# Weight preparation of a transformer block on eight cores: modulation weights in 1 MB slabs spread over the layer norm, the down-weight fold between attention heads, transposes behind them

## The chip, the cores and the metric

The program runs on all eight cores of one Trainium2 chip. Each core computes one of eight batch entries and holds its own copy of the weights; the cores don't exchange data. The metric is the device time of the slowest core in microseconds. A profile shows one execution, on the slowest core.

## The reference

One block: attention and a gated feed-forward part, each behind a layer norm that is modulated by a vector computed from `c`.

```python
mod = (_silu(L0_c) @ L0_wmod).reshape(8, 6, 1, -1)
sa, ca, ga, sb, cb, gb = (mod[:, k] for k in range(6))
ga = (2 * (ga >= 0) - 1) * jnp.maximum(jnp.abs(ga), 0.25)
gb = (2 * (gb >= 0) - 1) * jnp.maximum(jnp.abs(gb), 0.25)
h = _layernorm(x) * (1 + ca) + sa
x = x + ga * attention(h, w_qkv, w_out)      # 16 heads of 128, S = D = 2048
h = _layernorm(x) * (1 + cb) + sb
x = x + gb * ffn(h, gate_w, up_w, down_w, router_w1, router_w2)
# ffn: (silu(h @ gate.T) * (h @ up.T) * top-16-of-64 block mask) @ down.T, I = 8192
```

All inputs are float32; `wmod` is 2048 x 12288 (96 MB), `gate_w`, `up_w` and `down_w` are 64 MB each, `w_qkv` 48 MB, `w_out` 16 MB.

## The kernel before

The program is one long function, `build_nc`, that appends instructions to five lists, one per engine (TensorE "pe", ScalarE "act", VectorE "dve", SyncE "sp", GpSimd "gp"). Each engine works its list strictly in order; what stands later waits for what stands earlier. `b.wait` puts a semaphore wait into an engine's list. `b.dma(queue, ...)` issues a transfer from SP ("sp"), GpSimd ("gp") or ScalarE ("sc"); it first waits for the transfer that used the same of its queue's channels (7, 5 and 4, in turn), so at most that many are in flight per queue. Casts from float32 to bfloat16 in a DMA are issued by GpSimd. Eight PSUM banks are handed over by `bank_acquire`, `bank_written`, `bank_read` and `bank_read_done`.

The stages, in program order:

1. *Modulation* (L311 to L348). 24 column blocks of 512, each in 8 tiles of 256 rows: GpSimd loads a tile of `wmod` (512 KB of float32) into a ring of six, TensorE multiplies it with `silu(c)` (L338), VectorE copies the row into `mod_raw` (L343). After block 7, `replicate` (L290) spreads `ca` and `sa` over 128 partitions by a matmul with ones (L298). Behind it come the casts of `w_qkv` and `w_out` (L353, L355), the signs and magnitudes of `ga` and `gb` (L362 to L373), their way through `vec_scr` in HBM into `ga_cols` and `gb_cols`, and `cb1_rep` and `sb_rep`.
2. *First layer norm* (L437 to L461). 16 tiles of `x`, in groups of four: load, sum and squares, small statistics, then scale, shift and a transpose by TensorE (L426, copied out at L432).
3. *Casts* of `gate_w` and `up_w` to bfloat16 in HBM (L465 to L469), 32 of 4 MB, issued by GpSimd.
4. *The fold* (L474 to L489): `down_w` times `gb`, in 256 steps of 128 x 512. SP loads `wdf_in` (two buffers), VectorE multiplies (L486), GpSimd stores to `wd_bf`. In VectorE's list all 256 stand ahead of the first head.
5. *Preps* (L499 to L526), on SP alone: 192 pairs of a DMA transpose into `prep_buf` (from `wg_bf`, `wu_bf`, `wd_bf`) and a scatter to `wgT`, `wuT` or `wdT`. Each waits for the one ahead.
6. *Attention* (`emit_head`, L528), 16 heads. Every second head loads V weights and computes V (L546) for two heads; each head loads and computes Q and K (L569), then runs four quarters: scores (L594), exponentials on ScalarE (L603), the product with V (L617), and on VectorE the reciprocal and the scaling (L624, L627). The next quarter's scores can start only when VectorE has freed the four banks of the last one. The weight loads are issued by ScalarE.
7. *Output projection* (L660), the second sum and statistics (L684 to L707).
8. *Feed-forward part* (from L709). SP loads `router_w1` (L713); at L747 VectorE and ScalarE wait for all preps; then four strips of 512 tokens (L897, L904, L950).

Of the kernel before, what the change touches and what calls it, by code (L numbers as in the profile page):

```python
# [128 lines left out]
def build_nc(phases=4, taps=(), debug_sync=False):  # L129
# [95 lines left out]
    mod_raw = fv(A, 0, 12288, parts=1)  # L225
# [62 lines left out]


    def replicate(row_ap, dst_ap, dep_val, banks=(2, 3), plus1=False):  # L290
        last = None
        for j in range(4):
            bk = banks[j % 2]
# [15 lines left out]
        return last

    mm_t = {}  # L311
    mod_evac = []
    tile_idx = 0
    for nb_ in range(24):
        bk = nb_ % 2
        b.bank_acquire(bk)
        for kcp in range(8):
            slot = tile_idx % 6
            if tile_idx >= 6:
                b.wait("gp", "pe", mm_t[tile_idx - 6])  # L320
            src_ap = wmod_h[2 * kcp * 128:(2 * kcp + 2) * 128,
                            nb_ * 512:(nb_ + 1) * 512]
            src_ap = src_ap.rearrange("(two p) j -> p two j", p=128)
            dst_ap = wmod_ring[:, slot * 1024:(slot + 1) * 1024]
            dst_ap = dst_ap.rearrange("p (two j) -> p two j", two=2)
            t_d = b.dma("gp", dst_ap, src_ap)
            b.wait_tok("pe", t_d)
            if nb_ == 0 and kcp == 0:
                b.wait("pe", "act", t_siluc)
            for sub in range(2):  # L330
                kc = 2 * kcp + sub
                mm_t[tile_idx] = b.op(
                    "pe", lambda e, o=bank(bk)[0:1, :],
                    l=silu_cb[:, kc:kc + 1],
                    r=wmod_ring[:, slot * 1024 + sub * 512:
                                slot * 1024 + sub * 512 + 512],
                    s=(kc == 0), p=(kc == 15):
                    e.matmul(o, l, r, start=s, stop=p), "pe")  # L338
            tile_idx += 1
        b.bank_written(bk)  # L340
        b.bank_read("dve", bk)
        t = b.op("dve", lambda e, d=mod_raw[0:1, nb_ * 512:(nb_ + 1) * 512],
                 s=bank(bk)[0:1, :]: e.tensor_copy(d, s), "dve")  # L343
        b.bank_read_done("dve", bk)
        mod_evac.append(t)
        if nb_ == 7:
            t_ca1 = replicate(mod_ca, ca1_repA, mod_evac[7], plus1=True)
            t_sa = replicate(mod_sa, sa_repA, mod_evac[7])  # L348

    cast_order = [0, 2, 4, 1, 3, 5]  # L350
    cast_qkv_t = [None] * 6
    for ch in cast_order:
        cast_qkv_t[ch] = b.dma("gp", wqkv_bf[:, ch * 1024:(ch + 1) * 1024],  # L353
                               wqkv_h[:, ch * 1024:(ch + 1) * 1024])
    cast_wout_t = [b.dma("gp", wout_bf[:, ch * 1024:(ch + 1) * 1024],  # L355
                         wout_h[:, ch * 1024:(ch + 1) * 1024]) for ch in range(2)]

    sgn_scr = fv(R2, 0, 1024)[0:1, :]
    sgn2 = fv(R2, 2048, 1024)[0:1, :]
    abs_scr = fv(R2, 4096, 1024)[0:1, :]  # L360
    abs2 = fv(R2, 6144, 1024)[0:1, :]
    for row_base in (4096, 10240):  # L362
        for hf in range(2):
            seg = mod_raw[0:1, row_base + hf * 1024:row_base + (hf + 1) * 1024]
            b.op("dve", lambda e, r=seg: e.tensor_scalar(
                sgn_scr, r, 0.0, 2.0, OP.is_ge, OP.mult), "dve")
# [5 lines left out]
            b.op("dve", lambda e: e.tensor_scalar(abs2, abs_scr, 0.25, None, OP.max), "dve")
            b.op("dve", lambda e, r=seg: e.tensor_mul(r, sgn2, abs2), "dve")  # L373
    cb1_row = fv(R2, 0, 2048)[0:1, :]
    t_modpost = b.op("dve", lambda e: e.tensor_scalar(cb1_row, mod_cb, 1.0, None, OP.add), "dve")

    b.wait("act", "dve", t_modpost)
    t1 = b.dma("sc", vec_scr[0:1, :], mod_ga)
    t2 = b.dma("sc", vec_scr[1:2, :], mod_gb)
    b.wait_tok("sp", t1)  # L380
    b.wait_tok("sp", t2)
    b.dma("sp", ga_cols, vec_scr[0:1, :].rearrange("a (k p) -> (a p) k", p=128),
          slow_ok=True)
    t_gbcols = b.dma("sp", gb_cols,
                     vec_scr[1:2, :].rearrange("a (k p) -> (a p) k", p=128),
                     slow_ok=True)


    t_cb1 = replicate(cb1_row, cb1_rep, t_modpost)
    t_sbr = replicate(mod_sbv, sb_rep, t_modpost)  # L390

# [98 lines left out]
    t_wdfold = wdf_out_t[255]  # L490

    wgT_v = wgT_h.rearrange("(ic p dc) j -> ic p dc j", ic=NB, p=128)
    wuT_v = wuT_h.rearrange("(ic p dc) j -> ic p dc j", ic=NB, p=128)
    wdT_v = wdT_h.rearrange("(g c p s) j -> g c p s j", g=4, c=NB, p=128)
# [3 lines left out]
    last_scat = 0  # L498
    b.wait("sp", "dve", wdf_ts_t[255])  # L499
    for name, src_bf, dstv in (("wg", wg_bf, wgT_v), ("wu", wu_bf, wuT_v)):  # L500
        for dcq in range(NDC):
            for qu in range(4):
                need_ch = ((qu + 1) * 2048 - 1) // 512
                b.wait_toks("sp", [cast_t[(name, ch)] for ch in range(need_ch + 1)])
                b.wait_tok("sp", last_scat)
                t_tp = b.dma("sp", prep_buf,
                             src_bf[qu * 2048:(qu + 1) * 2048,
                                    dcq * 128:(dcq + 1) * 128],
                             transpose=True)
                b.wait_tok("sp", t_tp)  # L510
                dst = dstv[qu * 16:(qu + 1) * 16, :, dcq, :].transpose([1, 0, 2])
                src_ap = prep_buf.rearrange("p (ic j) -> p ic j", ic=16)
                last_scat = b.dma("sp", dst, src_ap)
                prep_gu_toks.append(last_scat)
        prep_t[name] = last_scat
    b.wait_toks("sp", wdf_out_t)
    for cq in range(NB):
        b.wait_tok("sp", last_scat)
        t_tp = b.dma("sp", prep_buf, wd_bf[:, cq * 128:(cq + 1) * 128],
                     transpose=True)  # L520
        b.wait_tok("sp", t_tp)
        dst = wdT_v[:, cq, :, :, :].transpose([1, 0, 2, 3])
        src_ap = prep_buf.rearrange("p (g s j) -> p g s j", g=4, s=4)
        last_scat = b.dma("sp", dst, src_ap)
        prep_wd_toks.append(last_scat)
    prep_t["wd"] = last_scat  # L526
# [537 lines left out]
```

How the kernel before makes its waits and increments, by code:

```python
        def f(e, sem=sem, val=val):  # L51
            e.wait_ge(sems[sem], val)
# [4 lines left out]
    def op(self, eng, fn, sem=None, n=1):  # L57
        if (self.debug_sync and eng in OWN_ALL) or eng in self.AUTO_SELF:
            own = OWN_ALL[eng]
            val = self.cnt[own]
            if val > 0:
                sems = self.sems
                self.emit(eng, lambda e, own=own, val=val:
                          e.wait_ge(sems[own], val))
        if sem is None:
            self.emit(eng, lambda e, fn=fn: fn(e))
            return None
        self.cnt[sem] += n
        tgt = self.cnt[sem]
        sems = self.sems
        def f(e, fn=fn, sem=sem, n=n):
            fn(e).then_inc(sems[sem], n)
        self.emit(eng, f)
        return tgt
```

## Time and profile before

| | us |
|---|---|
| median of the runs shown | 8954.16 (8994.57 and 8913.74) |
| the profiled execution, its own time | 8727.57 |
| span of its slowest core (core 4) | 8726.0 |
| spans of the eight cores | 8653.6 to 8726.0 |
| TensorE busy | 5271.0 (60%) |
| VectorE, ScalarE busy | 1438.4, 1057.0 |
| mean granted TensorE clock | 0.789 of full speed |

A span runs from the first to the last instruction of a core. The busy share is an average over stages that differ much, so the stages are read one by one. DMA share is the mean busy share of the core's 16 DMA engines. The two runs without a profile took some 2 to 3% longer than the profiled one.

### The profile page before, as it was taken

How to read it: one execution, taken by the hardware profiler on the slowest of the kernel's cores; microseconds unless marked ns; L12 is line 12 of the kernel's file. 1: busy time of each engine (PE TensorE's matmuls, PEld its weight loads, DVE VectorE, ACT ScalarE, POOL GpSimd, SP SyncE). 2: the span in 40 equal slices, each digit the busy share in tenths (PEclk: the TensorE clock that was granted, in tenths of full speed). 3: DMA queues.
4: the chain of work that ended last, by engine and by line, in shares of the span. 5: the costliest groups of instructions: out<-in, count | busy, mean ns of one | idle time of the engine just before them, and what ended most of it. 6: DMA issues, size and time to landing. Idle time of an engine off the chain costs nothing.

```text
span 8726.0 us, 77823 instructions; the slowest of 8 cores (8653.6 to 8726.0 us)
## 1 busy us (share of the span) xinstructions
PE 5271.0 (60%) x25265; PEld 2409.3 (28%) x25265; DVE 1438.4 (16%) x2507; ACT 1057.0 (12%) x1239; POOL 301.3 (3%) x499
## 2 busy tenths in 40 slices
PE   5410011006666676666615888768886888858888
PEld 0000010003433444433202333323333333323333
DVE  0152001220000000001044211131102212031110
ACT  0010000003433333431110000000000000000000
POOL 3200001220000000000000000000000000000000
PEclk8555556558888888887856999879997899979999
DMA  9999996566666655300021223322232222422234
GB/s 130 141 148 118 109 110 146 175 182 128 128 127 130 130 129 143 94 10 15 22 80 49 106 102 115 117 77 102 102 127 76 106 102 102 140 68 102 102 111 135
DMA packets 1158830, 945.75 MB, mean 108 GB/s; under 512 B 791666, under 2 KB 1021106, under 8 KB 1152178
## 3 DMA queue, kind: packets, MB, share of 16 engines
q1 hardware_dynamic: 945408, 672.28, 27.1%
q0 software_dynamic: 83632, 184.59, 15.8%
q10 hardware_dynamic: 129412, 83.91, 3.5%
q8 instruction: 228, 3.74, 0.2%
q14 instruction: 150, 1.23, 0.1%
HBM read 839.97 MB, written 251.67 MB: 125 GB/s over the span
## 4 chain that ended last, share of the span: by engine, by line
PE 53%; DMA 15%; DVE 11%; another core or an unknown queue 7%; issue 7%; ACT 5%; DVEq 1%; ACTq 0%; POOLq 0%; POOL 0%; SPq 0%
PE PS L897 13%; PE PS L950 10%; PE PS L904 10%; PE PS L569 6%; DMA wd_bf<-A 4%; ACT A L603 4%; DMA R<-wmod 4%; PE PS L660 3%; PE PS L617 3%; DMA A<-wqkv_bf 2%; PE PS L546 2%; DMA R<-x 2%; PE PS L594 2%; DVE dout_tile L916 2%
## 5 line engine op out<-in xcount | busy, mean ns | idle before, releaser
L897 PE MATMUL PS<-A 128*128 128x512 bf16 x4096 | 1119.1, 435 | 5.9 <-DMA A<-wgT 5.8
L950 PE MATMUL PS<-R,A 128*128 128x512 bf16 x4096 | 916.2, 387 | 51.1 <-DMA A<-wdT 31.9
L904 PE MATMUL PS<-A 128*128 128x512 bf16 x4096 | 925.8, 379 | 0.0
L594 PE MATMUL PS<-A 128*128 128x512 bf16 x1024 | 376.0, 475 | 879.9 <-DVE R L627 661.1
L603 ACT ACTIVATE A<-PS,cexp 128x1024 bf16<-128x1024 f32 x512 | 616.7, 1204 | 944.2 <-PE PS L594 904.9
L569 PE MATMUL PS<-R,A 128*128 128x512 bf16 x2048 | 514.7, 418 | 283.6 <-DMA A<-wqkv_bf 283.6
L897 PEld LDWEIGHTS PS<-A 128*128 128x128 bf16 x4096 | 426.2, 109 | 648.4 <-issue 336.0
L546 PE MATMUL PS<-A,R 128*128 128x256 bf16 x2048 | 241.0, 283 | 577.6 <-DMA A<-wqkv_bf 576.4
L950 PEld LDWEIGHTS PS<-R,A 128*128 128x128 bf16 x4096 | 406.2, 100 | 558.4 <-issue 96.9
L904 PEld LDWEIGHTS PS<-A 128*128 128x128 bf16 x4096 | 400.7, 98 | 483.4
L916 DVE TENSOR_TENSOR dout_tile<-silu_sb,PS 128x512 bf16<-128x512 bf16 x256 | 176.1, 688 | 1835.7 <-PE PS L904 1777.1
L911 ACT ACTIVATE silu_sb<-PS 128x512 bf16<-128x512 f32 x256 | 152.9, 597 | 2517.0 <-PE PS L897 2444.0
L594 PEld LDWEIGHTS PS<-A 128*128 128x128 bf16 x1024 | 103.5, 103 | 1109.8 <-issue 1047.7
L546 PEld LDWEIGHTS PS<-A,R 128*128 128x128 bf16 x2048 | 207.3, 102 | 610.5 <-issue 579.1
L569 PEld LDWEIGHTS PS<-R,A 128*128 128x128 bf16 x2048 | 214.0, 106 | 580.1 <-issue 385.0
L860 PE MATMUL PS<-mask_fm,id64b 64*1 64x512 bf16 x256 | 105.7, 413 | 444.0 <-DVE R L921 441.5
L617 PE MATMUL PS<-A 128*128 128x129 bf16 x4096 | 334.4, 251 | 31.5 <-ACT A L603 31.5
L624 DVE RECIPROCAL inv<-PS 128x1 f32<-128x1 f32 x256 | 43.1, 168 | 1845.0 <-PE PS L617 1824.8
L617 PEld LDWEIGHTS PS<-A 128*128 128x128 bf16 x4096 | 316.5, 115 | 65.2 <-issue 57.5
L660 PE MATMUL PS<-R,A 128*128 128x512 bf16 x1024 | 267.5, 421 | 67.6 <-DMA A<-wout_bf 66.9
L486 DVE TENSOR_SCALAR A<-A,gb_cols 128x512 bf16<-128x512 f32 x256 | 124.7, 487 | 1075.3 <-DMA wd_bf<-A 1071.2
L338 PE MATMUL PS<-R,silu_cb 128*1 128x512 bf16 x384 | 192.9, 608 | 168.1 <-DMA R<-wmod 156.3
(125 smaller groups left out, 2416.6 us busy)
## 6 DMA issues: line engine op xcount, KB each, us to landing
A<-wgT SPq DMA_DIRECT2D x256, 512.0 KB, 3.6
A<-wuT SPq DMA_DIRECT2D x256, 512.0 KB, 4.5
A<-wdT SPq DMA_DIRECT2D x128, 1024.0 KB, 5.4
A<-down_w SPq DMA_DIRECT2D x256, 256.0 KB, 3.0
R<-wmod POOLq DMA_DIRECT2D x192, 256.0 KB, 8.6
wg_bf<-gate_w POOLq DMA_DIRECT2D x16, 2048.0 KB, 97.4
wu_bf<-up_w POOLq DMA_DIRECT2D x16, 2048.0 KB, 96.9
wd_bf<-A POOLq DMA_DIRECT2D x256, 128.0 KB, 3.0
```

Of the source, the lines that this page charges most:

```text
L338: e.matmul(o, l, r, start=s, stop=p), "pe")
L546: e.matmul(o, l, r, start=s, stop=p), "pe")
L569: e.matmul(o, l, r, start=s, stop=p), "pe")
L594: e.matmul(o, l, r, start=True, stop=True), "pe")
L603: e.activation(d, s, AF.Exp, bias=cexp[:, 0:1], scale=cexp[:, 1:2]), "act")
L617: e.matmul(o, l, r, start=s, stop=p), "pe")
L660: e.matmul(o, l, r, start=s, stop=p), "pe")
L897: e.matmul(o, l, r, start=s, stop=p), "pe")
L904: e.matmul(o, l, r, start=s, stop=p), "pe")
L911: e.activation(silu_sb, s, AF.Silu), "act")
L916: e.tensor_mul(dout_tile, silu_sb, s), "dve")
L950: e.matmul(o, l, r, start=s, stop=p), "pe")
```

## The change

The change reorders the preparation of weights and vectors.

- The modulation is computed in six groups of 2048 columns, each in 16 slabs of 128 rows x 2048 columns (1 MB of float32). The ring has two slots. A slab feeds four matmuls into four banks (L304). `repl_from_banks` copies each bank's row to a bounce buffer and replicates it; `gagb_post` does signs and magnitudes straight from the banks, in four pieces, each stored through `vec_scr` from ScalarE's queue.
- `sa` and `ca` (32 slabs) come first. The 32 slabs of `ga` and `sb` stand in the layer norm, two behind each tile of `x`. The 32 of `cb` and `gb` follow, with three casts of `w_qkv` between them. The other casts come behind slab 95.
- The fold becomes `wdf_step`, 20 steps behind each head from head 2 on. Its store is issued by SP, no longer by GpSimd.
- The preps become `emit_preps`, called behind the last head and the last fold step.

```diff
-    for nb_ in range(24):
-        bk = nb_ % 2
-        b.bank_acquire(bk)
-        for kcp in range(8):
-            slot = tile_idx % 6
...
+    def mod_slab_dma(idx):
+        if idx >= 2:
+            b.wait("gp", "pe", slab_mm[idx - 2])
+        g, kc = divmod(idx, 16)
+        slab_tok[idx] = b.dma("gp", ring_slot(idx),
+                              wmod_h[kc * 128:(kc + 1) * 128,
+                                     g * 2048:(g + 1) * 2048])
...
+            b.wait("act", "dve", b.cnt["dve"])
+            if q > 0:
+                b.wait_tok("act", toks[q - 1])
+            b.op("act", lambda e, s=src: e.activation(abs_scr, s, AF.Abs), "act")
...
+    for idx in range(16):
+        mod_slab_dma(idx)
+        mod_slab_mms(idx)
+    t_bounce_pe = repl_from_banks(sa_repA, False, 0)
...
             tm_tile_to_fm(h_tm, R1v, i, t_app)
+            for s2 in range(2):
+                mod_slab_dma(32 + 2 * i + s2)
+                mod_slab_mms(32 + 2 * i + s2)
+            if i == 7:
+                toks_ga = gagb_post(0, t_bounce_pe)
...
-    for k in range(256):
+    def wdf_step(k):
         dc, part = k // 16, k % 16
         pp = k % 2
+        if k == 0:
+            b.wait_tok("dve", t_gbcols)
         if k >= 2:
             b.wait("sp", "dve", wdf_ts_t[k - 2])
         t_in = b.dma("sp", wdf_in[pp],
...
-        b.wait("gp", "dve", wdf_ts_t[k])
-        wdf_out_t[k] = b.dma("gp", wd_bf[dc * 128:(dc + 1) * 128,
+        b.wait("sp", "dve", wdf_ts_t[k])
+        wdf_out_t[k] = b.dma("sp", wd_bf[dc * 128:(dc + 1) * 128,
                                          part * 512:(part + 1) * 512], wdf_out[pp])
...
+    def emit_preps():
+        last_scat = 0
+        b.wait("sp", "dve", wdf_ts_t[255])
...
     if phases >= 2:
+        wdf_k = 0
         for h in range(H):
             emit_head(h)
+            if h >= 2:
+                while wdf_k < min(256, (h - 1) * 20):
+                    wdf_step(wdf_k)
+                    wdf_k += 1
+        while wdf_k < 256:
+            wdf_step(wdf_k)
+            wdf_k += 1
         t_attn_dve = b.cnt["dve"]
+        emit_preps()
```

GpSimd's list, from the first load of `wmod` on, before:

```order
12 L89 DMA R<-wmod 128x2x512 x192
13 L89 DMA wqkv_bf<-w_qkv 2048x1024 x6
14 L89 DMA wout_bf<-w_out 2048x1024 x2
15 L89 DMA wg_bf<-gate_w 64x16384 x16
16 L89 DMA wu_bf<-up_w 64x16384 x16
17 L89 DMA wd_bf<-A 128x512 x256
```

and with the change:

```order
12 L89 DMA R<-wmod 128x2048 x72
13 L89 DMA wqkv_bf<-w_qkv 2048x1024 x2
14 L89 DMA R<-wmod 128x2048 x16
15 L89 DMA wqkv_bf<-w_qkv 2048x1024
16 L89 DMA R<-wmod 128x2048 x8
17 L89 DMA wqkv_bf<-w_qkv 2048x1024 x3
18 L89 DMA wout_bf<-w_out 2048x1024 x2
19 L89 DMA wg_bf<-gate_w 64x16384 x16
20 L89 DMA wu_bf<-up_w 64x16384 x16
```

Three casts of `w_qkv` moved between the slabs, and the stores of the fold left this list.

VectorE's list between the layer norm and the first head, before:

```order
144 L432 COPY R<-PS 128x4x128 x4
145 L486 TENSOR_SCALAR A<-A,gb_cols 128x512 x256
146 L624 RECIPROCAL inv<-PS 128x1
147 L627 TENSOR_SCALAR R<-PS,inv 128x128
148 L624 RECIPROCAL inv<-PS 128x1
```

and with the change, where head 3 ends and head 4 begins (the first 20 fold steps stand in the same way between heads 2 and 3):

```order
289 L651 RECIPROCAL inv<-PS 128x1
290 L654 TENSOR_SCALAR R<-PS,inv 128x128
291 L514 TENSOR_SCALAR A<-A,gb_cols 128x512 x20
292 L651 RECIPROCAL inv<-PS 128x1
293 L654 TENSOR_SCALAR R<-PS,inv 128x128
```

The block of 256 multiplies is cut into pieces of 20 that stand between heads.

SP's list ahead of the first transpose (`A` is `wdf_in`, `wdf_out` or `prep_buf`), before:

```order
3 L89 DMA A<-down_w 128x512 x256
4 L84 DMA_TRANSPOSE A<-wg_bf 128x2048
5 L89 DMA wgT<-A 128x16x128
6 L84 DMA_TRANSPOSE A<-wg_bf 128x2048
7 L89 DMA wgT<-A 128x16x128
```

and with the change:

```order
511 L89 DMA A<-down_w 128x512
512 L89 DMA wd_bf<-A 128x512
513 L89 DMA A<-down_w 128x512
514 L89 DMA wd_bf<-A 128x512
515 L84 DMA_TRANSPOSE A<-wg_bf 128x2048
516 L89 DMA wgT<-A 128x16x128
```

The fold's loads and stores alternate on SP, and the transposes still stand behind the last of them.

## Rows read from the trace of the kernel before

**Rows 1.** Busy time by stage: stretch, length, each engine's busy time, clock, DMA share, GB/s
```profile
0.00:380.00 380.00, 206.82 (x400) 27.35 (x400) 24.00 (x40) 2.77 (x4) 143.15 (x208) 0.70 1.03 136
380.00:740.00 360.00, 48.15 (x272) 28.36 (x272) 185.93 (x201) 37.31 (x40) 5.08 (x7) 0.50 1.02 140
740.00:1368.00 628.00, 30.20 (x256) 25.79 (x256) 0.25 (x1) 6.20 (x16) 15.15 (x30) 0.52 0.98 109
1368.00:1936.00 568.00, 41.72 (x208) 19.92 (x208) 125.55 (x262) 15.69 (x17) 137.92 (x254) 0.54 0.57 176
1936.00:3634.00 1698.00, 1149.71 (x7367) 667.44 (x7367) 108.00 (x416) 602.96 (x619) 0.00 (x0) 0.83 0.60 131
3634.00:4593.00 959.00, 536.15 (x2922) 266.93 (x2922) 169.74 (x313) 197.28 (x219) 0.00 (x0) 0.78 0.11 30
4593.00:8726.00 4133.00, 3258.30 (x13841) 1373.56 (x13841) 824.95 (x1277) 194.79 (x325) 0.00 (x0) 0.88 0.30 102
```

**Rows 2.** DMA issues: tile, queue, count, KB each at the destination, median us to landing
```profile
A<-down_w SPq DMA_DIRECT2D x256, 256.0 KB, 3.0
R<-wmod POOLq DMA_DIRECT2D x192, 256.0 KB, 8.6
...
wd_bf<-A POOLq DMA_DIRECT2D x256, 128.0 KB, 3.0
...
R<-x ACTq DMA_DIRECT2D x16, 1024.0 KB, 13.6
...
A<-wout_bf ACTq DMA_DIRECT2D x16, 512.0 KB, 4.2
```

**Rows 3.** GpSimd's DMA issues at L89: ns min/median/max, first and last start in us
```profile
L89 POOL DMA_DIRECT2D R<-wmod x192: 698/710/742, 5.3 to 362.3; - x192
L89 POOL DMA_DIRECT2D wg_bf<-gate_w x16: 501/501/507, 566.4 to 965.5; - x16
L89 POOL DMA_DIRECT2D wu_bf<-up_w x16: 501/501/501, 984.5 to 1279.0; - x16
L89 POOL DMA_DIRECT2D wqkv_bf<-w_qkv x6: 1017/1022/1058, 363.6 to 417.2; - x6
L89 POOL DMA_DIRECT2D wout_bf<-w_out x2: 1017/1017/1017, 467.2 to 521.0; - x2
```

**Rows 4.** Modulation on TensorE: the group of L338, and two replications
```profile
L338 PE MATMUL PS<-R,silu_cb 128*1 128x512 bf16 x384 | 192.9, 608 | 168.1 <-DMA R<-wmod 156.3 <-ACT silu_cb L287 11.8
...
130.53 13.99 PE L298 MATMUL PS<-A,ones_f 1*128 1x512 f32 x16 [1.00 <-DVE A L343]
```

**Rows 5.** Timeline, first weight loads of head 0: start, duration, instruction, [idle before <-releaser]
```profile
732.49 0.39 ACTq L89 DMA_DIRECT2D A<-wqkv_bf  x1
...
1252.23 27.63 PE L546 MATMUL PS<-A,R 128*128 128x256 bf16 x234 [519.94 <-DMA A<-wqkv_bf]
...
1369.59 15.28 PE L569 MATMUL PS<-R,A 128*128 128x512 bf16 x64 [85.97 <-DMA A<-wqkv_bf]
```

**Rows 6.** Timeline, head 0: first and second quarter's scores on TensorE
```profile
1411.73 1.15 PE L594 MATMUL PS<-A 128*128 128x512 bf16 x4 [0.89 <-ACT A L573]
...
1936.18 1.86 PE L594 MATMUL PS<-A 128*128 128x512 bf16 x4 [509.12 <-DVE R L627]
```

**Rows 7.** Timeline of VectorE: start of heads 2 and 3, end of head 14
```profile
2196.47 0.17 DVE L624 RECIPROCAL inv<-PS 128x1 f32<-128x1 f32 x1 [96.86 <-PE PS L617]
...
2308.89 0.17 DVE L624 RECIPROCAL inv<-PS 128x1 f32<-128x1 f32 x1 [55.61 <-PE PS L617]
...
3830.05 0.35 DVE L627 TENSOR_SCALAR R<-PS,inv 128x128 bf16<-128x128 f32 x1
```

**Rows 8.** Timeline of SP: first transpose, last scatter, the load behind it
```profile
1933.24 2.65 SPq L84 DMA_TRANSPOSE A<-wg_bf  x1
...
3629.92 0.36 SPq L89 DMA_DIRECT2D wdT<-A  x1
4593.45 0.34 SPq L89 DMA_DIRECT2D A<-router_w  x1
```

More of the change, by code:

```diff
@@ L223, in build_nc @@
     R2v = R2.rearrange("p (c t) -> p c t", c=16)
-    mod_raw = fv(A, 0, 12288, parts=1)
     PT = A[:, 0:4096]
@@ L287, in build_nc, with ring_slot, mod_slab_mms, repl_from_banks @@
     t_siluc = b.op("act", lambda e: e.activation(silu_cb, c_sb, AF.Silu), "act")
[L290 to L293, printed above, removed]
+    slab_tok = {}
+    slab_mm = {}
+    def ring_slot(idx):
+        return R2[:, (idx % 2) * 2048:(idx % 2) * 2048 + 2048]
+    def mod_slab_dma(idx):
[5 more added lines that the diff above has]
+                                     g * 2048:(g + 1) * 2048])
+    def mod_slab_mms(idx):
+        g, kc = divmod(idx, 16)
+        slot = ring_slot(idx)
+        b.wait_tok("pe", slab_tok[idx])
+        if idx == 0:
+            b.wait("pe", "act", t_siluc)
+        for q in range(4):
+            if kc == 0:
+                b.bank_acquire(q)
+            b.op("pe", lambda e, o=bank(q)[0:1, :], l=silu_cb[:, kc:kc + 1],
+                 r=slot[:, q * 512:(q + 1) * 512], s=(kc == 0), p=(kc == 15):
+                 e.matmul(o, l, r, start=s, stop=p), "pe")
+            if kc == 15:
+                b.bank_written(q)
+        slab_mm[idx] = b.cnt["pe"]
+    bounce = [fv(R2, 4096 + 1024 * j, 512)[0:1, :] for j in range(4)]
+    def repl_from_banks(dst_ap, plus1, pe_guard, dma_guard=None):
+        if pe_guard:
+            b.wait("dve", "pe", pe_guard)
+        if dma_guard is not None:
+            b.wait_tok("dve", dma_guard)
+        cp_t = [0] * 4
+        for q in range(4):
+            b.bank_read("dve", q)
+            cp_t[q] = b.op("dve", lambda e, d=bounce[q], s=bank(q)[0:1, :]:
+                           e.tensor_copy(d, s), "dve")
+            b.bank_read_done("dve", q)
+        for q in range(4):
+            bk = 6 + q % 2
             b.bank_acquire(bk)
-            b.wait("pe", "dve", dep_val)
-            b.op("pe", lambda e, o=bank(bk), l=ones_f,
-                 r=row_ap[0:1, j * 512:(j + 1) * 512]:
+            b.wait("pe", "dve", cp_t[q])
+            b.op("pe", lambda e, o=bank(bk), l=ones_f, r=bounce[q]:
                  e.matmul(o, l, r, start=True, stop=True), "pe")
@@ L301, in replicate @@
             if plus1:
-                last = b.op("dve", lambda e, d=dst_ap[:, j * 512:(j + 1) * 512],
-                            s=bank(bk):
-                            e.tensor_scalar(d, s, 1.0, None, OP.add), "dve")
-            else:
-                last = b.op("dve", lambda e, d=dst_ap[:, j * 512:(j + 1) * 512],
-                            s=bank(bk): e.tensor_copy(d, s), "dve")
+                b.op("dve", lambda e, d=dst_ap[:, q * 512:(q + 1) * 512],
+                     s=bank(bk): e.tensor_scalar(d, s, 1.0, None, OP.add), "dve")
+            else:
+                b.op("dve", lambda e, d=dst_ap[:, q * 512:(q + 1) * 512],
+                     s=bank(bk): e.tensor_copy(d, s), "dve")
@@ L308, in replicate @@
             b.bank_read_done("dve", bk)
[L309 to L313, printed above, removed]
-    for nb_ in range(24):
-        bk = nb_ % 2
-        b.bank_acquire(bk)
-        for kcp in range(8):
-            slot = tile_idx % 6
[L319 to L366, printed above, removed]
+        return b.cnt["pe"]
+    def gagb_post(row, pe_guard):
+        sgn_scr, sgn2, abs_scr, abs2 = bounce
+        if pe_guard:
+            b.wait("dve", "pe", pe_guard)
+            b.wait("act", "pe", pe_guard)
+        toks = []
+        for q in range(4):
+            b.bank_read("dve", q)
+            b.bank_read("act", q)
+            src = bank(q)[0:1, :]
+            b.op("dve", lambda e, s=src: e.tensor_scalar(
+                sgn_scr, s, 0.0, 2.0, OP.is_ge, OP.mult), "dve")
@@ L369, in build_nc @@
             b.wait("act", "dve", b.cnt["dve"])
-            b.op("act", lambda e, r=seg: e.activation(abs_scr, r, AF.Abs), "act")
+            if q > 0:
+                b.wait_tok("act", toks[q - 1])
+            b.op("act", lambda e, s=src: e.activation(abs_scr, s, AF.Abs), "act")
             b.wait("dve", "act", b.cnt["act"])
[L372 to L390, printed above, removed]
+            b.op("dve", lambda e: e.tensor_scalar(abs2, abs_scr, 0.25, None,
+                                                  OP.max), "dve")
+            b.op("dve", lambda e: e.tensor_mul(abs_scr, sgn2, abs2), "dve")
+            b.wait("act", "dve", b.cnt["dve"])
+            toks.append(b.dma("sc", vec_scr[row:row + 1, q * 512:(q + 1) * 512],
+                              abs_scr))
+            b.bank_read_done("dve", q)
+            b.bank_read_done("act", q)
+        return toks
+    for idx in range(16):
+        mod_slab_dma(idx)
+        mod_slab_mms(idx)
+    t_bounce_pe = repl_from_banks(sa_repA, False, 0)
+    for idx in range(16, 32):
+        mod_slab_dma(idx)
+        mod_slab_mms(idx)
+    t_bounce_pe = repl_from_banks(ca1_repA, True, t_bounce_pe)
+    cast_qkv_t = [None] * 6
     def ln_group_math(st, g):
@@ L461, in build_nc @@
             tm_tile_to_fm(h_tm, R1v, i, t_app)
+            for s2 in range(2):
[3 more added lines that the diff above has]
+                toks_ga = gagb_post(0, t_bounce_pe)
+                b.wait_toks("sp", toks_ga)
+                b.dma("sp", ga_cols, vec_scr[0:1, :].rearrange(
+                    "a (k p) -> (a p) k", p=128), slow_ok=True)
     t_h_done_pe = b.cnt["pe"]
     t_h_done_dve = b.cnt["dve"]
+    t_bounce_pe = repl_from_banks(sb_rep, False, t_bounce_pe,
+                                  dma_guard=toks_ga[3])
+    for idx in range(64, 80):
+        mod_slab_dma(idx)
+        mod_slab_mms(idx)
+        if idx == 71:
+            for ch in (0, 2):
+                cast_qkv_t[ch] = b.dma(
+                    "gp", wqkv_bf[:, ch * 1024:(ch + 1) * 1024],
+                    wqkv_h[:, ch * 1024:(ch + 1) * 1024])
+    t_bounce_pe = repl_from_banks(cb1_rep, True, t_bounce_pe)
+    for idx in range(80, 96):
+        mod_slab_dma(idx)
+        mod_slab_mms(idx)
+        if idx == 87:
+            cast_qkv_t[4] = b.dma("gp", wqkv_bf[:, 4 * 1024:5 * 1024],
+                                  wqkv_h[:, 4 * 1024:5 * 1024])
+    toks_gb = gagb_post(1, t_bounce_pe)
+    b.wait_toks("sp", toks_gb)
+    t_gbcols = b.dma("sp", gb_cols,
+                     vec_scr[1:2, :].rearrange("a (k p) -> (a p) k", p=128),
+                     slow_ok=True)
+    b.wait_toks("dve", toks_gb)
+    for ch in (1, 3, 5):
+        cast_qkv_t[ch] = b.dma("gp", wqkv_bf[:, ch * 1024:(ch + 1) * 1024],
+                               wqkv_h[:, ch * 1024:(ch + 1) * 1024])
+    cast_wout_t = [b.dma("gp", wout_bf[:, ch * 1024:(ch + 1) * 1024],
+                         wout_h[:, ch * 1024:(ch + 1) * 1024]) for ch in range(2)]
     cast_t = {}
@@ L486, in build_nc @@
                            e.tensor_scalar(o, i, sc, None, OP.mult), "dve")
-        b.wait("gp", "dve", wdf_ts_t[k])
-        wdf_out_t[k] = b.dma("gp", wd_bf[dc * 128:(dc + 1) * 128,
+        b.wait("sp", "dve", wdf_ts_t[k])
+        wdf_out_t[k] = b.dma("sp", wd_bf[dc * 128:(dc + 1) * 128,
                                          part * 512:(part + 1) * 512], wdf_out[pp])
[L490 to L494, printed above, removed]
+    def emit_preps():
+        last_scat = 0
+        b.wait("sp", "dve", wdf_ts_t[255])
+        for name, src_bf, dstv in (("wg", wg_bf, wgT_v), ("wu", wu_bf, wuT_v)):
+            for dcq in range(NDC):
+                for qu in range(4):
+                    need_ch = ((qu + 1) * 2048 - 1) // 512
+                    b.wait_toks("sp", [cast_t[(name, ch)]
+                                       for ch in range(need_ch + 1)])
+                    b.wait_tok("sp", last_scat)
+                    t_tp = b.dma("sp", prep_buf,
+                                 src_bf[qu * 2048:(qu + 1) * 2048,
+                                        dcq * 128:(dcq + 1) * 128],
+                                 transpose=True)
+                    b.wait_tok("sp", t_tp)
+                    dst = dstv[qu * 16:(qu + 1) * 16, :, dcq, :].transpose([1, 0, 2])
+                    src_ap = prep_buf.rearrange("p (ic j) -> p ic j", ic=16)
+                    last_scat = b.dma("sp", dst, src_ap)
+                    prep_gu_toks.append(last_scat)
+            prep_t[name] = last_scat
+        b.wait_toks("sp", wdf_out_t)
+        for cq in range(NB):
+            b.wait_tok("sp", last_scat)
+            t_tp = b.dma("sp", prep_buf, wd_bf[:, cq * 128:(cq + 1) * 128],
+                         transpose=True)
+            b.wait_tok("sp", t_tp)
+            dst = wdT_v[:, cq, :, :, :].transpose([1, 0, 2, 3])
+            src_ap = prep_buf.rearrange("p (g s j) -> p g s j", g=4, s=4)
+            last_scat = b.dma("sp", dst, src_ap)
+            prep_wd_toks.append(last_scat)
+        prep_t["wd"] = last_scat
     prep_t = {}
@@ L497, in build_nc @@
     prep_wd_toks = []
[L498 to L526, printed above, removed]
     def emit_head(h):
```

13 lines of the change are left out of this document (3 added, 10 removed).

## The prediction

> **What bounds the kernel now.** I read the busy time by stage first [rows 1], then the queue that ends last in each. The stages are: modulation (0 to 380 us), first layer norm (to 740), an almost empty stretch (to 1368, TensorE busy 30 us of 628), the fold of `down_w` (to 1936, TensorE busy 42 of 568), attention (to 3634 and on to about 3940), output projection and second statistics (to 4593), and the feed-forward part, 4133 us at a granted clock of 0.88. The two empty stretches cost 1200 us. In the first, DMA share is 0.98: the casts of the weights run, and the load of the first V weights, issued at 732.5, lets TensorE go on only at 1252.2, after 519.9 us; the next load lands as the last cast does, at 1369.6 [rows 5]. In the second TensorE waits 509.1 us for VectorE [rows 6], because all 256 fold steps stand ahead of the first head's normalisation.
>
> What the change must not disturb is SP. Its 192 transpose-and-scatter pairs begin at 1933.2 and the last is issued at 3629.9; SP next issues `router_w` at 4593.5 [rows 8]. So about 960 us of slack separate the end of that chain (3634) from the point where it is needed. The chain takes 1701 us, 8.9 us per pair, strictly one after the other.
>
> **When the casts can start.** POOL's old tiles leave at (362.3 - 5.3)/191 = 1.9 us each [rows 3], at DMA share 1.03 [rows 1], 8.6 us to landing with five in flight [rows 2]. A new slab is two old tiles and only two slabs are in flight: landing at least 4 x 1.9 = 7.6 us, then four matmuls of 0.6 [rows 4] and 0.7 of issue [rows 3], 11 us per pair of slabs, so 5.5 us per slab. Bounds: 3.8 (the old byte rate kept) and 8.3 (a 1 MB slab lands as slowly as 1 MB of `x` did beside casts, 13.6 [rows 2]: (13.6 + 3.1)/2).
> Here stands a rule of the Trainium skill, page "DMA: Bandwidth & Descriptors", section "Anatomy of one DMA": a DMA costs about 2.0 us plus bytes over 436 GB/s. By it a 1 MB slab lands in 4.4 us and the cadence is 3.7. The rows, 8.6 us for half of it at a full DMA share, speak against it; by the page the sum below would be about 115 us less.
> - `sa` and `ca`: 7 + 32 x 5.5 + two replications of about 10 us (two took 14.0 of TensorE [rows 4] and now each has four copies ahead) = 203.
> - Layer norm with 32 slabs between: per tile the greater of VectorE's 186/16 = 11.6 us [rows 1] and two slabs, 11; per group of four some 16 more for the last load of `x` and the small statistics; 62 x 4 = 248, plus 30 for the `ga` work, whose four small stores wait for one another: 483.
> - 32 slabs more, 176, two replications, 20, and three casts of 8 MB ahead of slabs in POOL's order. Two casts of 4 MB take 39 us (`wu`: (1279.0 - 984.5)/15 = 19.6 each); 8 MB beside loads of `x` about 50 (467.2 to 521.0) [rows 3]. I take 41: 123. So the remaining casts start at 483 + 176 + 20 + 123 = 800 us, against 363.6 before.
> - Then 5 x 41 + 32 x 19.5 = 830: the casts end at 1630, not 1368.
>
> **Head 0.** Its V load is issued at about 850 and meets the same casts: 520 us, then 30 us of V, then the Q load, which lands with the end of the casts, as the old one did. The old casts ended at the stage boundary of 1368 [rows 1]; the first score matmul came 44 us later, at 1411.7 [rows 6]. A quarter of a head's attention is about (128 - 56)/4 = 18 us, where 128 is (3830 - 1936)/14.75 heads and 56 the gap below. The second quarter starts at 1692 against 1936.2: attention is 244 us early. That is all that remains of 509 us of removed stall.
>
> **The fold between heads.** The old step takes 568/254 = 2.2 us, with loads issued ahead from SP and stores from POOL. Now SP issues load, waits for VectorE, issues the store, and only then the next load. A step is 3.0 us landing [rows 2], 0.5 multiply, two issues of 0.35 on SP: 4.2 us. Twenty steps hold VectorE 84 us after each head from 2 on. TensorE queues behind them at the second quarter of the next head, which needs the banks that VectorE frees. The idle room is 96.9 us ahead of an even head and 55.6 ahead of an odd one [rows 7]. So even heads pay nothing, odd ones 28: six of them up to the end of head 14, 168 us. Bounds per step: 3.1 (nearly nothing is paid) and 6.0 (one transfer of each kind, both waited for). I take 4.2, since the transfers overlap.
> The Trainium skill, same page, section "Issuing engines are not separate DMA queues", says that moving a DMA to another issuing engine saves or costs only sequencer time. By that the step stays 2.2 us, 44 us per head, and the 168 go. I follow the waits that the rows show, not this.
> The head loads no longer share with the transposes: `wout` lands in 4.2 us, as these might [rows 2]; some 30 loads gain 1 us, -30.
>
> **The preps.** They now follow fold step 255, which follows head 14. VectorE ended head 14 at 3830.1 [rows 7]. Now: 3830 - 244 + 168 - 30 = 3724, plus 16 steps of 4.2, 67: 3791. The 192 pairs, 1701 us, end at 5492. Before, they lay beside attention at no cost; that cover is now gone but for projection and statistics. SP's `router_w` load comes behind them at 5492, not 4593, and everything from there is unchanged: 4133 us. Pair bounds: 8.3 us (no loads beside) and 9.1.
> Sum: 3791 + 1701 + 4133 = 9625 against a span of 8726: +899. The profiled execution took 8727.6, so 9627 by its own measure. The runs shown have a median of 8954, 226 above it; the added 899 us are DMA time that a TensorE clock does not touch, so I add it to the median: 9853 us.
>
> **Rivals.**
> 1. *Fold steps at 6 us.* For: each step holds two transfers of 3.0 that SP issues in turn. Against: SP does not wait for the store itself. Price: 120 us per head, 64 for odd and 23 for even heads, in place of 28 and 0: 6 x 36 + 6 x 23 + 29 = +383, 10236 us.
> 2. *Slabs at 8.3 us,* because two in flight are too few. For: 13.6 us for 1 MB of `x`. Against: that was beside casts. Price 64 x 2.8 outside the norm and half of that per slab inside, +225, 10078 us.
> 3. *Head loads are not held by the casts* (other casts, other strides). Against: 519.9 us [rows 5]. Then head 0's second quarter starts at 951 (850, load 15, V 30, Q and K 38, a quarter 18), heads 0 to 2 pass by about 1340 with slower loads, but fold loads beside casts need at least the 13.6 us of an `x` load [rows 2], and 20 of them with store fill the time to the casts' end. Head 3 goes on at 1650 where it was 2320 (1936 + 3 x 128): 670 early instead of 244, one odd stall of 28 less: 9625 - 454 = 9171, or 9399 us.
> 4. *Not slower:* neither loads nor fold steps are held by casts. Place: the queues of ACT and SP between 850 and 1630. The second quarter at 951 is then 985 us ahead of 1936: the preps start at 3830 - 985 + 168 - 30 + 67 = 3050 and the span is 8884, +158, 9112 us, 1.8% more. It decides from a start of the preps before 3068 us (2% of 8727.6). DMA share 0.98 to 1.02 in all old stretches with casts speaks against it.
> That the preps end behind attention is in all four, since one wait on SP orders them.
>
> **How the numbers follow.** Forecast 0.66; rival 1 0.13; rival 2 0.10; rival 3 0.08; rival 4 0.03. The forecast's own bounds (cadence -120 to +225, fold -180 to +383, pairs -110 to +40, and whether 226 us of offset belongs on top) seldom fall together. I set 9390 to 10180: it holds rivals 2 and 3 and most of the forecast, and leaves out rivals 1 and 4. A measurement of this kernel can tell about 2%. Slower by over 2%: 0.96; within 2%: 0.03 (rival 4); faster 0.01.
>
> **What would show it.** Right: POOL's `wg` casts from about 900 to 1630; the V load of head 0 outstanding some 500 us; odd heads with about 28 us of TensorE waiting for VectorE; first transpose on SP near 3790, last near 5490; an almost empty TensorE between about 4400 and 5490 with VectorE waiting for the last `wdT` scatter. Wrong: a first transpose before 3100, transposes well under 8 us a pair, or fold steps near 2 us.

## The result and the profile after

The kernel is slower. Its median is 9470.7 us (9300.1 to 9781.4, 11 runs) against 8971.5 us (8727.5 to 9095.6, 10 runs) for the kernel before. The ratio is 1.063, 95% interval 1.057 to 1.070. In some executions, six of the eleven with the change, the cores of one die or of both show a lower granted clock and take some per cent longer; the medians hold these too, while the ratios and the spans compared here are of the others (whose median with the change is 9315.1). The profiled execution took 9319.5 us, and its span is 9317.9 us against 8726: 592 us more. The forecast of the span was 9625 (+899).

Busy time by stage of the kernel with the change, in the columns of [rows 1]; the stages are cut where its own work changes:

```profile
180.00:500.00 320.00, 111.89 (x424) 39.99 (x424) 167.95 (x183) 27.00 (x31) 23.23 (x42) 0.54 0.66 119
500.00:660.00 160.00, 47.91 (x96) 10.57 (x96) 5.48 (x8) 0.00 (x0) 14.05 (x25) 0.50 0.86 121
660.00:1480.00 820.00, 108.14 (x712) 65.41 (x712) 17.06 (x48) 53.14 (x61) 19.64 (x36) 0.56 0.99 112
...
1593.00:3570.00 1977.00, 1257.22 (x8142) 740.84 (x8143) 248.34 (x723) 649.85 (x672) 0.00 (x0) 0.81 0.24 66
3570.00:4210.00 640.00, 309.12 (x1460) 133.18 (x1459) 120.45 (x152) 72.03 (x92) 0.00 (x0) 0.76 0.68 145
4210.00:5182.00 972.00, 0.00 (x0) 0.00 (x0) 18.91 (x56) 6.11 (x9) 0.00 (x0) 0.50 0.57 129
5182.00:9318.00 4136.00, 3259.63 (x13841) 1374.98 (x13841) 824.47 (x1275) 194.78 (x325) 0.00 (x0) 0.88 0.31 102
```

From the load of `router_w` on, nothing changed: 4136 us here, 4133 before. All of the loss lies ahead of it, and most of it can be seen in one row: from 4210 to 5182 TensorE executes nothing. In [rows 1] no stage of zero existed; the two nearly empty ones there (628 and 568 us) are now partly filled, and this one took more than they gave back. What fills the 972 us is in SP's groups, which answer to [rows 8]:

```profile
L84 SPq DMA_TRANSPOSE A<-wg_bf x64: 1262/1956/4414, 3501.6 to 4098.6; - x64
L84 SPq DMA_TRANSPOSE A<-wu_bf x64: 1262/2008/2801, 4110.0 to 4672.1; - x64
L84 SPq DMA_TRANSPOSE A<-wd_bf x64: 1262/2024/2567, 4680.3 to 5177.3; - x64
...
L89 SPq DMA_DIRECT2D A<-router_w x1: 346/346/346, 5182.3 to 5182.3; - x1
```

The pairs run from 3501.6 to 5182, 1680 us, 8.75 us each (forecast 1701 and 8.9). They began at 1933.2 before. The load of `router_w` now follows the last pair at once, where it used to come 960 us behind it. The list of waits names the two ends of this (engine, line waited for: us in all, times, longest), beside two waits of attention:

```profile
PE PS L766 <- DVE A L753: 1146.1, 1, 1146.1
DVE A L752 <- DMA A<-router_w: 944.5, 1, 944.5
DVE A L514 <- DMA A<-down_w: 927.7, 243, 5.8
...
PE PS L596 <- DMA A<-wqkv_bf: 757.3, 32, 503.1
...
PE PS L621 <- DVE R L654: 324.1, 48, 32.7
```

The first is the consequence, the second the cause: VectorE wants `router_w`, and the instruction that loads it stands behind the pairs on SP. The third shows the fold step: 243 of 256 multiplies wait for their own load. The last holds what TensorE pays for it. Of its 324 us, 48 waits of 3.2 us (154) are the ordinary ones of a quarter, as the experiment with fold stores from GpSimd shows below; some 170 are paid for the fold steps, where [rows 6] had one wait of 509.

Head 0's weight loads, in TensorE's timeline, are where the forecast missed ([rows 5, 6] before):

```profile
752.57 30.30 PE L573 MATMUL PS<-A,R 128*128 128x256 bf16 x256 [84.50 <-DMA A<-wqkv_bf]
836.82 16.73 PE L596 MATMUL PS<-R,A 128*128 128x512 bf16 x64 [53.95 <-DMA A<-wqkv_bf]
1356.65 16.23 PE L596 MATMUL PS<-R,A 128*128 128x512 bf16 x64 [503.10 <-DMA A<-wqkv_bf]
...
1392.16 1.87 PE L621 MATMUL PS<-A 128*128 128x512 bf16 x4 [3.18 <-DVE R L654]
```

V waited 84.5 us, Q 54 and K 503. The second quarter starts at 1392, not at 1692. GpSimd's issues say why V and Q came through:

```profile
L89 POOL DMA_DIRECT2D R<-wmod x96: 527/528/553, 5.3 to 658.0; - x96
L89 POOL DMA_DIRECT2D wg_bf<-gate_w x16: 498/498/507, 704.2 to 1089.0; - x16
L89 POOL DMA_DIRECT2D wu_bf<-up_w x16: 498/498/501, 1107.8 to 1398.4; - x16
L89 POOL DMA_DIRECT2D wqkv_bf<-w_qkv x6: 1015/1029/1043, 445.2 to 660.6; - x6
L89 POOL DMA_DIRECT2D wout_bf<-w_out x2: 1015/1015/1015, 662.3 to 666.7; - x2
```

V was fetched from 698 on, beside the last casts of `w_qkv` and `w_out`. The first `gate_w` cast was issued at 704.2 and landed only 192.6 us later, when the last casts of `w_out`, which stand ahead of it, were done (GpSimd waited for the last one until 878). K was asked for at 854.4, behind Q, and met `gate_w` and `up_w`.

### The profile page after: what moved, and what is told of

It is laid out like the page before. It is cut to its first block, busy times and chain, and to the rows that moved or that the text cites. A ratio compares the mean times of both kernels' runs of the same rounds, so it can differ in the third digit from the quotient of the medians.

```text
span 9317.9 us, 77188 instructions; the slowest of 8 cores (9285.2 to 9317.9 us)
## 1 busy us (share of the span) xinstructions
PE 5241.2 (56%) x25265; PEld 2421.0 (26%) x25265; DVE 1435.4 (15%) x2514; ACT 1057.4 (11%) x1243; POOL 77.7 (1%) x147
## 4 chain that ended last, share of the span: by engine, by line
PE 45%; DMA 27%; DVE 10%; another core or an unknown queue 8%; issue 5%; ACT 4%; SPq 1%; DVEq 1%; ACTq 0%; POOL 0%; POOLq 0%
PE PS L933 12%; PE PS L986 10%; PE PS L940 10%; DMA A<-down_w 4%; ACT A L630 3%; DMA A<-wg_bf 3%; DMA A<-wd_bf 3%; PE PS L596 3%; DMA A<-wu_bf 3%; DMA wuT<-A 3%; DMA wgT<-A 3%; DMA R<-wmod 3%; PE PS L573 3%; PE PS L644 2%
## 5 line engine op out<-in xcount | busy, mean ns | idle before, releaser
L986 PE MATMUL PS<-R,A 128*128 128x512 bf16 x4096 | 917.7, 388 | 51.6 <-DMA A<-wdT 32.7
L621 PE MATMUL PS<-A 128*128 128x512 bf16 x1024 | 370.9, 471 | 546.0 <-DVE R L654 324.1
L304 PE MATMUL PS<-R,silu_cb 128*1 128x512 bf16 x384 | 176.8, 618 | 285.5 <-DMA R<-wmod 285.3
```

## The experiments

**Modulation and cast order alone.** The fold goes back ahead of the heads, in one piece with stores from GpSimd, and the preps in front of the heads.

```diff
-            emit_head(h)
-            if h >= 2:
-                while wdf_k < min(256, (h - 1) * 20):
...
-        emit_preps()
+        for wdf_k in range(256):
+            wdf_step(wdf_k)
+        emit_preps()
+        for h in range(H):
+            emit_head(h)
```

> One part of the change alone: slabs and cast order as changed; fold (stores from GpSimd) and preps stand ahead of the heads again, as before. Theory (the preps behind attention are the loss): casts end near 1480 us instead of 1368, so fold, attention and everything behind end about 112 us later: span 8840 (+1.3% against before), preps off the path, SP idle some 950 us ahead of router_w. Rival (slabs and cast order are themselves the loss): span near 9300.

Measured: 8881.7 and 9199.8 us, span 8880.2. SP's groups:

```profile
L84 SPq DMA_TRANSPOSE A<-wg_bf x64: 1262/1938/3997, 2106.0 to 2667.9; - x64
...
L84 SPq DMA_TRANSPOSE A<-wd_bf x64: 1262/1952/4370, 3252.3 to 3778.5; - x64
L89 SPq DMA_DIRECT2D A<-router_w x1: 345/345/345, 4752.3 to 4752.3; - x1
```

The slack of 970 us behind the pairs is back, so in this kernel they lie off the path. What is left, +154 us, is the price of the new modulation and cast order: the pairs start 173 later, 122 of which is the fold's own later start (VectorE's steady run of multiplies begins at 1489.8, before at 1367.8); the other 51 are told in the last section.

**Fold and preps alone.** The modulation, layer norm and cast order of before; the changed fold and preps.

```diff
-    for idx in range(16):
-        mod_slab_dma(idx)
-        mod_slab_mms(idx)
...
+    for nb_ in range(24):
+        bk = nb_ % 2
+        b.bank_acquire(bk)
...
```

> The other part alone: modulation and casts as before; fold steps between heads, preps behind. Theory: second quarter of head 0 at 1429 instead of 1936 (507 early), six odd stalls of 30, so the first transpose comes near 3540; +1680 of preps, +4133: span 9355, slower than before by 7%. Rival (the loss needs the new casts): span at or under 8726.

Measured: median 9555.8 us (9273.4 to 9638.0, 4 runs), span 9271.8; its groups and waits:

```profile
L84 SPq DMA_TRANSPOSE A<-wg_bf x64: 1262/2026/5160, 3478.8 to 4062.0; - x64
...
L89 SPq DMA_DIRECT2D A<-router_w x1: 346/346/346, 5136.4 to 5136.4; - x1
```

```profile
PE PS L550 <- DMA A<-wqkv_bf: 557.5, 8, 512.3
...
PE PS L598 <- DVE R L631: 324.1, 48, 32.7
```

The fold and the preps cost 546 of the 592 us. The span came out 83 us under the expected one and the first transpose 61 under; the rival is out. The new modulation adds only 46 on top, against 154 by itself. Of these, 23 lie ahead of the first transpose and 23 in the pairs, which differ by as much between cores of one execution (1658 us on core 5 with the change, 1680 on core 3). The last cast is issued at 1398.4 with the new order and at 1264.5 with the old one, but what waits for the end of the casts with the new order is head 1: its Q begins at 1483.3, and here at 1463.9. The V load waits 512 us here, as in [rows 5]: with the old order it meets `gate_w`, with the new it does not.

**Fold stores from GpSimd.**

```diff
-        b.wait("sp", "dve", wdf_ts_t[k])
-        wdf_out_t[k] = b.dma("sp", wd_bf[dc * 128:(dc + 1) * 128,
+        b.wait("gp", "dve", wdf_ts_t[k])
+        wdf_out_t[k] = b.dma("gp", wd_bf[dc * 128:(dc + 1) * 128,
```

> The change, with the fold's store issued by GpSimd, so that SP can load ahead. Theory (the step is long because SP waits between load and store): step 2.2 us instead of 4.3, 44 us per head, no odd stalls; first transpose some 200 us earlier (near 3300), span 9110. Rival (the step is long because of the transfer itself or of what else runs): step stays above 4, span 9318.

Measured: 9384.8 to 9701.0 us, four runs, which are not compared; the profile is read from cores 4 to 7, whose granted clock (0.773 to 0.778) was that of the change, and the rows are of core 5. VectorE's timeline with the change:

```profile
1733.64 0.49 DVE L514 TENSOR_SCALAR A<-A,gb_cols 128x512 bf16<-128x512 f32 x1
1737.96 0.49 DVE L514 TENSOR_SCALAR A<-A,gb_cols 128x512 bf16<-128x512 f32 x1 [3.84 <-DMA A<-down_w]
...
1815.41 0.49 DVE L514 TENSOR_SCALAR A<-A,gb_cols 128x512 bf16<-128x512 f32 x1 [3.76 <-DMA A<-down_w]
```

and of this experiment:

```profile
1739.27 1.08 DVE L514 TENSOR_SCALAR A<-A,gb_cols 128x512 bf16<-128x512 f32 x2
1743.80 1.08 DVE L514 TENSOR_SCALAR A<-A,gb_cols 128x512 bf16<-128x512 f32 x2 [3.45 <-DMA wd_bf<-A]
1748.46 1.08 DVE L514 TENSOR_SCALAR A<-A,gb_cols 128x512 bf16<-128x512 f32 x2 [3.58 <-DMA wd_bf<-A]
```

With SP's store the multiplies come one by one, (1815.41 - 1733.64)/19 = 4.3 us apart, each waiting for its load. With GpSimd's they come in twos, 4.6 us per two, and wait for the store of two steps ago. The wait of TensorE for VectorE's banks falls from a longest of 32.7 us to 3.5, and from 324.1 us in all to 153.6:

```profile
PE PS L621 <- DVE R L654: 153.6, 48, 3.5
```

The first transpose stands at 3333.2 instead of 3492.0 on the same core, and cores 4 to 7 end at 9088.8 to 9122.0 us instead of 9285.4 to 9316.8, about 200 us earlier. So the queue of one store is worth some 200 us of the loss. The transfers themselves got no shorter (median from issue to landing on core 5: 3.1 us for a load and 3.4 for a store, against 2.8 and 1.8 with the change). What went is SP's wait for VectorE ahead of the store, behind which the next load stands. The Trainium skill, page "DMA: Bandwidth & Descriptors", section "Issuing engines are not separate DMA queues", says that DMAs started from several engines run on the same DMA engines, and that only the sequencer's time to start them is saved. That agrees with the landings here and leaves out the wait in the queue, which is what counted.

**Casts as blocks of 1024 columns.** The same 4 MB per cast, as 1024 rows of 1024 columns in place of 512 whole rows (the profile calls the whole rows 64x16384: they are one stretch of memory).

```diff
-            cast_t[(name, ch)] = b.dma("gp", dst[ch * 512:(ch + 1) * 512, :],
-                                       src[ch * 512:(ch + 1) * 512, :])
+            rr = slice((ch // 2) * 1024, (ch // 2 + 1) * 1024)
+            cc = slice((ch % 2) * 1024, (ch % 2 + 1) * 1024)
+            cast_t[(name, ch)] = b.dma("gp", dst[rr, cc], src[rr, cc])
```

> The change, with the 32 casts of gate_w and up_w as blocks of 1024 rows x 1024 columns (same 4 MB each) instead of 512 full rows. In the changed kernel head 0's V and Q loads took 84 and 54 us beside casts of w_qkv and w_out, and its K load 503 us beside casts of gate_w. Theory (the shape of the casts' rows decides how long a head load is held): K load of head 0 under 100 us, casts still end near 1480, heads 0 to 2 partly done by then, first transpose some 200 us earlier, span 9100. Rival (any running cast holds it, by bytes): K load near 500 us, span 9318.

Measured: median 9433.4 us (9054.7 to 9597.3, 3 runs), span 9053.1. The load of K, and the casts' issues:

```profile
911.61 15.41 PE L597 MATMUL PS<-R,A 128*128 128x512 bf16 x64 [56.75 <-DMA A<-wqkv_bf]
```

```profile
L89 POOL DMA_DIRECT2D wg_bf<-gate_w x16: 748/748/757, 706.7 to 1105.7; - x16
L89 POOL DMA_DIRECT2D wu_bf<-up_w x16: 748/748/760, 1126.7 to 1426.3; - x16
```

K waits 56.8 us instead of 503.1. The casts go at nearly the same rate, (1426.3 - 1126.7)/15 = 20.0 us each against 19.4; their last issue is 28 us later. The stretch in which they run, in the columns of the first fence:

```profile
660.00:1480.00 820.00, 275.19 (x1796) 162.01 (x1797) 31.57 (x104) 139.95 (x152) 29.58 (x38) 0.67 1.00 113
```

TensorE is busy 275 us of it, where the change had 108, at a DMA share of 1.00 against 0.99. What held the head loads was the form of the casts beside them, not a full DMA. The span falls by 265 us.

The trace also shows how. These are the queues of GpSimd (q0) and ScalarE (q10) while the load of K is out, as packets, MB and share of the engines, first with the change (857 to 1356 us), then of this experiment (858 to 911):

```profile
q0 software_dynamic: 2457, 54.65, 99.3%
q10 hardware_dynamic: 2063, 0.52, 0.7%
...
q0 software_dynamic: 2665, 5.38, 89.3%
q10 hardware_dynamic: 2064, 0.52, 7.4%
```

The load is 2063 or 2064 packets, as the profile counts them, of some 250 bytes both times, and beside it the casts moved 1.2 or 1.3 packets for each of its own. But a packet of a whole-row cast is 22 KB (54.65 MB in 2457, with the end of `w_out` in it), and one of a narrow cast 2 KB. The old V load is the same picture at twice the bytes: 2064 packets of 1.05 MB in all, 2216 of 25 KB beside it, 735 to 1252 in the kernel before. That is why 512 KB and 1 MB waited alike: by these counts the wait follows the number of the load's packets and the size of the cast's.

The same edit in the kernel before, whose fold stands ahead of the first normalisation:

> The kernel before, with the narrow casts of gate_w and up_w alone. Theory: head 0's V load takes about 55 us instead of 520, but head 0 still stops at its second quarter until all 256 fold steps are done, and these wait for the end of the casts; so TensorE only waits elsewhere, and the time stays: 8727 within 1%. Rival (the held loads cost time by themselves): 300 to 500 us less.

Measured over three rounds: ratio to before 1.002 (0.999 to 1.005). Its timeline of TensorE:

```profile
790.63 30.22 PE L547 MATMUL PS<-A,R 128*128 128x256 bf16 x256 [59.92 <-DMA A<-wqkv_bf]
...
942.67 16.88 PE L570 MATMUL PS<-R,A 128*128 128x512 bf16 x64 [53.45 <-DMA A<-wqkv_bf]
...
1973.46 1.87 PE L595 MATMUL PS<-A 128*128 128x512 bf16 x4 [997.68 <-DVE R L628]
```

The wait for V fell by 460 us, and the wait for VectorE grew from 509 to 998. The fast load is worth something only once the fold has left the place ahead of head 0, which the change does.

**Preps between the heads too.** 19 fold steps with stores from GpSimd, then ten `wg` and `wu` pairs, behind each head from head 1 on; the `wd` pairs behind attention.

```diff
+            if h >= 1 and wdf_k < 256:
+                b.wait_tok("sp", prep_state["scat"])
+                for _ in range(min(19, 256 - wdf_k)):
+                    wdf_step(wdf_k)
+                    wdf_k += 1
+                b.wait("sp", "dve", wdf_ts_t[wdf_k - 1])
+                for _ in range(min(10, 128 - prep_state["n"])):
+                    gu_prep()
...
-        emit_preps()
+        wd_preps()
```

> The change, with the wg and wu pairs of the preps spread over the heads (10 behind the 19 fold steps of each head from head 1 on), the fold's store from GpSimd, and only the 64 wd pairs behind attention. Theory (the loss is the serial chain on SP behind attention, nothing else): no odd stalls, attention ends near 3440, the wd pairs end near 3980 inside projection and statistics, router_w is issued near 4090, span 8220, 12% under the change and 6% under before. Rival (the feed-forward part cannot start earlier, or transposes beside the fold cost as much as they hide): span 8700 or more.

Measured: median 8343.2 us (8341.9 to 8346.5), ratio to before 0.947 (0.936 to 0.958), span 8341.7.

```profile
L84 SPq DMA_TRANSPOSE A<-wg_bf x64: 1262/1994/4394, 1659.1 to 2549.4; - x64
...
L84 SPq DMA_TRANSPOSE A<-wd_bf x64: 1262/2094/3827, 3466.4 to 4012.2; - x64
L89 SPq DMA_DIRECT2D A<-router_w x1: 346/346/346, 4212.1 to 4212.1; - x1
```

The pairs end 200 us ahead of `router_w`: off the path again. It is 120 us above what was expected. Stalls that I had counted as gone are still there, 90 us of them beyond the ordinary 153.6; the waits show that a piece's first `down_w` load stands behind ten pairs on SP:

```profile
DVE A L514 <- DMA A<-down_w: 440.3, 19, 50.6
PE PS L622 <- DVE R L655: 243.9, 48, 28.5
```

**Both together, with the new and with the old modulation.** The first takes the kernel just told, with the narrow casts, from head 2 on, 20 steps and ten pairs. The second is the same with the modulation and cast order of before.

```diff
-            if h >= 1 and wdf_k < 256:
+            if h >= 2 and wdf_k < 256:
...
-                for _ in range(min(19, 256 - wdf_k)):
+                for _ in range(min(20, 256 - wdf_k)):
```

> The one before, with the narrow casts of gate_w and up_w as well, and fold and pairs from head 2 on (20 and 10). Theory: the head loads stay near 55 us under casts instead of 500, so head 4 starts near 1610; attention ends near 3190, span 7980. Rival: the casts now meet fold steps and lose what the loads gained; span 8220.

```diff
-    for idx in range(16):
-        mod_slab_dma(idx)
-        mod_slab_mms(idx)
...
+    for nb_ in range(24):
+        bk = nb_ % 2
...
```

> The one before, with the modulation and cast order of before (tiles of 512 KB, ring of six, casts from 364 us on). Theory (the new modulation order costs about 110 us at the end of the casts): casts end near 1370 instead of 1480, span 50 to 110 us less, 7900. Rival (the new modulation order pays once the loads are no longer held): span above that of e6.

The fastest executions took 8171.6 and 8191.2 us; the expected 7980 and 7900 were both missed by 190 us and more. In the first, 125 us are again waits of TensorE for VectorE's banks beyond the ordinary 154 (278.6 in all); the rest was not followed. Three runs of each could not tell them apart. So both ran once more, side by side:

> The kernel of e6 once more, beside the one below on the same chip. If the new order of modulation and casts costs what it delays the casts by, about 110 to 150 us, this one is slower than the one below by that; if it is made up for by the earlier start of head 0, the two are equal within 0.5% (8170 us).

> The kernel of e7 once more, beside the one above. 8050 if the old order of modulation and casts is worth 110 to 150 us here; 8170 to 8190 if it is worth nothing.

Measured: new order 8150.5 us (8121.9 to 8710.2, 5 runs), ratio to before 0.931 (0.925 to 0.938); old order 8145.3 us (8106.6 to 8675.3, 4 runs), ratio 0.928 (0.920 to 0.935). The intervals overlap: beside a fold between the heads and narrow casts, the order of the modulation makes no difference that these runs can tell. Both kernels are about 7% faster than before, and the first takes 12% less than the change (0.931/1.063).

## Why the prediction came out as it did

The direction and the mechanism were right; the number was 382 us too high (9853 against 9470.7) and inside the range. 307 of that is the span (9625 against 9318, so that the loss was put at 899 and is 592), 75 the offset of the median above the span, put at 228 (9853 - 9625; 226 above the execution's own time) and here 153 (9471 - 9318). The offset was taken over and not worked out from the kernel. That the number lies inside the range is luck in that part: the profiled execution, which has next to no offset, took 9319 us, 71 under the lower end of 9390.

- **Preps on the path: right.** Taking them off again gave back 780 us in the span beyond what the store gave (9122.0 to 8341.7, with the fold also one head earlier). That the pairs take 1701 us: 1680. That the rest is unchanged: 4136 against 4133.
- **Fold step 4.2 us, odd stalls of 28: right.** 4.3 us, and TensorE's longest wait there is 32.7 us where the same wait is 3.5 with GpSimd's store. All these waits together fell by 324.1 - 153.6 = 170 us, where I had 168.
- **Head 0: wrong, and this is the step of the sum that failed.** I put the V load at "the same casts: 520 us", from one row [rows 5], and let the Q load land with the casts' end. The old V load had met `gate_w` casts; the moved one met `w_qkv` and `w_out` casts, and waited 84.5 us. The narrow casts show that the form of the cast decides: 503 against 57 us at nearly the same rate. First scores came 106 us ahead of the end of the casts, where I had 44 behind it: 150 us.
- **Start of the remaining casts at 800: 141 us too late.** The first of them was issued at 659. Half of this lies ahead of the last 32 slabs: `ca` was spread at 164 (forecast 203) and the layer norm ended at about 412 (forecast 483, though its own terms add up to 481). Behind it slabs came 4.1 us apart, not 5.5: 32 of them, 45 us less. The three casts between them held the slabs twice, for 76.7 and 37.2 us by the waits, 114 against 123; and the two replications added some 5 us each, where I had 10. In the first stretch slabs did come 5.0 us apart (issues at 20.17, 30.16 and 40.21, one for every second slab), close to the 5.5.
- These 150 and 141, and 10 for the casts' own 820 us instead of 830, are the 300 us by which the second quarter was early, and with them the first transpose: 3501.6 against 3791. The other terms behind it cancel within 15 us.
- **Rivals.** 1 (fold steps of 6 us) and 2 (slabs of 8.3) fell by these rows. 3 (loads not held) was true of V and Q but not of K, whose 503 us bound head 0; the span that it gave, 9171, lies 147 us below the measured one, nearer than the forecast, which lies 307 above. 4 fell. The narrow casts make the kernel that rival 3 described, at a span of 9053, 118 below what it gave.
- **The rule of the Trainium skill on the time of one DMA,** page "DMA: Bandwidth & Descriptors", section "Anatomy of one DMA", by which a slab lands in 4.4 us: the median landing is 6.7, between it and my 7.6 or more, while the cadence of 4.1 lies nearer to its 3.7.

## What to carry to other kernels

When a chain of transfers is moved, look at what stands behind it on its queue: here 1680 us of pairs ahead of one small load turned a hidden chain into 970 us of idle TensorE, and cutting it into pieces behind each head hid it again. A store that waits for another engine, put on the queue that issues the loads, puts that wait into every load; a queue that has nothing to prefetch is its place. And a wait of 500 us for a small load beside casts should be read together with the form of those casts, down to the bytes per packet of both queues, before it is carried over to another place.

## What the runs showed of the hardware

- Loads of narrow column blocks from ScalarE's queue (512 KB and 1 MB at the destination) waited 489 to 520 us beside casts of whole rows, and 53 to 60 us beside casts of the same 4 MB in pieces of 1024 columns, with the casts at 19 to 20 us each in both. It held in the change and in the kernel before. A load of either size is some 2064 packets; beside it the casts moved 1.1 to 1.3 packets for each of these, whether theirs were 25 KB or 2 KB. The Trainium skill, page "DMA: Bandwidth & Descriptors", section "Queues, rings and completion order", says that a DMA engine takes turns between its queues packet by packet; turns of about one to one agree with it.
- Narrow casts cost GpSimd 748 ns per issue against 498; the casts themselves went at 20.0 us each against 19.4.
- In the first experiment the fold ran at (2105.2 - 1489.8)/250 = 2.46 us per step against 2.2 before. The cause was not found; it is some 50 of its 154 us.
